# Second self attention: the second part of context, key and value weights filled with zeros to 128 rows

## The reference

```python
HEADS, DIM_HEAD, ATTN_MATRIX_SCALE = 8, 128, 1.5      # context: 2 x 512 rows of 192 features
qh = _split_heads(x @ Wq)                             # Wq 256 x 1024; 8 heads, 2048 x 128 each
kh = _split_heads(context @ Wk)                       # Wk 192 x 1024; 8 heads, 1024 x 128 each
vh = _split_heads(context @ Wv)                       # Wv 192 x 1024
sim = einsum('hid,hjd->hij', qh, kh) * DIM_HEAD ** -0.5
mean = mean(sim, axis=-1)
sim = (sim - mean) * 1.5 + mean
attn = softmax(sim, axis=-1)
out = einsum('hij,hjd->hid', attn, vh)                # heads side by side: 2048 x 1024
x = x + out @ Wout + bout
```

## Time and profile before

| what | value |
|---|---|
| median of three runs | 3127.7 us (3121.81 to 3133.32) |
| profiled execution, its span | 3124.2 us; no time is recorded for it beside the span |
| this part, its own block | from about 1627 us to about 2308 us of the span |
| TensorE busy | 2720.5 us, 87% |
| VectorE busy | 1999.9 us, 64% |
| ScalarE busy | 1747.3 us, 56% |
| GpSimd busy | 792.9 us, 25% |

### The profile page before, as it was taken

One profiled execution on the slowest core, in us unless ns is written; L12 is line 12 of the kernel. 1 busy time (PEld: TensorE's weight loads), 2 busy tenths in 40 slices (PEclk: granted clock), 3 DMA queues, 4 the chain that ended last, 5 costly groups with the idle time before them and its releaser, 6 DMA issues. The chain is left out here.

```text
span 3124.2 us, 50399 instructions
## 1 busy us (share of the span) xinstructions
PE 2720.5 (87%) x17384; PEld 2036.1 (65%) x17384; DVE 1999.9 (64%) x4360; ACT 1747.3 (56%) x3237; POOL 792.9 (25%) x887
## 2 busy tenths in 40 slices
PE   6778888888876689999979999999979999949998
PEld 3344444444435556777658888888867777748887
DVE  4788778778865756655646666666666556545444
ACT  3888887878874444444435555555555555542221
POOL 1122212222210134444432111111005566610000
PEclk8789889988878899999999999999989999969999
DMA  3000000000001111111010000000010000020000
GB/s 102 4 4 4 0 3 3 0 3 3 1 1 52 68 46 24 24 29 42 21 34 13 6 6 3 6 1 1 1 66 8 8 5 5 2 95 7 3 7 30
DMA packets 88677, 57.76 MB, mean 18 GB/s; under 512 B 55120, under 2 KB 78544, under 8 KB 88016
## 3 DMA queue, kind: packets, MB, share of 16 engines
q1 hardware_dynamic: 88528, 55.80, 6.0%
HBM read 39.00 MB, written 8.39 MB: 15 GB/s over the span
## 5 line engine op out<-in xcount | busy, mean ns | idle before, releaser
L672 DVE SCALAR_TENSOR_TENSOR a_w<-a_w,a_sinks 128x384 f32<-128x384 f32 x512 | 332.8, 715 | 32.0 <-ACT a_w L507 32.0
L2033 POOL TENSOR_SCALAR x_weights<-x_weights,x_sums 128x256 f32<-128x256 f32 x256 | 231.8, 924 | 275.0 <-DVE x_sums L2092 275.0
L1125 POOL TENSOR_SCALAR f_weights<-f_weights,f_sums 128x256 f32<-128x256 f32 x256 | 232.0, 924 | 272.9 <-DVE f_sums L1355 272.9
L486 ACT ACTIVATE a_e<-psum 128x1024 f32<-128x1024 f32 x192 | 195.4, 1018 | 155.7 <-PE psum L345 114.7
L1283 ACT ACTIVATE f_weights<-psum,f_negmax 128x256 f32<-128x256 f32 x256 | 117.7, 472 | 215.2 <-DVE f_negmax L1349 215.2
L1619 ACT ACTIVATE a_turned_w_hi<-psum 128x512 fp32r<-128x512 f32 x256 | 139.1, 596 | 152.0 <-PE psum L1529 151.9
L687 DVE SCALAR_TENSOR_TENSOR a_w<-a_e,psum 128x512 f32<-128x512 f32 x256 | 162.8, 677 | 92.8 <-ACT a_e L488 88.0
L342 PE MATMUL psum<-a_qT,a_kT_half 32*128 32x512 f32 x512 | 165.8, 727 | 60.4 <-DVE a_w L687 49.3
L488 ACT ACTIVATE a_e<-a_e 128x1024 f32<-128x1024 f32 x192 | 202.9, 1057 | 6.1
L2003 ACT ACTIVATE x_weights<-x_masked_s,x_negmax 128x256 f32<-128x256 f32 x256 | 127.0, 497 | 138.6 <-DVE x_negmax L2084 138.6
L1735 DVE TENSOR_REDUCE a_negmax<-psum 128x1 f32<-128x1024 f32 x128 | 156.7, 1224 | 65.7 <-PE psum L123 61.5
(11 more groups left out here) (361 smaller groups left out, 7725.5 us busy)
## 6 DMA issues: line engine op xcount, KB each, us to landing
f_xnT<-all_xnT_all SPq DMA_DIRECT2D x16, 256.0 KB, 2.3
f_pv_rows<-f_pv SPq DMA_DIRECT2D x8, 512.0 KB, 3.1
f_pv_groups<-f_pv_rows SPq DMA_DIRECT2D x8, 512.0 KB
f_w<-in_f_w SPq DMA_DIRECT2D x2, 2048.0 KB, 10.0
all_x_all<-in_x SPq DMA_DIRECT2D x1, 2048.0 KB, 8.4
a_xnT<-all_xnT_all SPq DMA_DIRECT2D x8, 256.0 KB, 2.3
x_xnT<-all_xnT_all SPq DMA_DIRECT2D x8, 256.0 KB, 2.3
x_ctxT<-in_x_ctxT SPq DMA_DIRECT2D x8, 256.0 KB, 2.7
```

What stands on the lines that cost most here:

```text
L486: act.activation(e[:, x, :], psS[x], ACT.Exp).then_inc(exp_done, 1)
L672: ins = dve.scalar_tensor_tensor(part, part, sinks[:, col:col + 1], part, ALU.is_ge, ALU.mult)
L1125: ins = pool.tensor_scalar(w, w, sums[:, k, h, t:t + 1], None, ALU.mult)
L2033: ins = pool.tensor_scalar(w, w, sums[:, k, h, t:t + 1], None, ALU.mult)
```

## The change

The second chunk of the context, of the key weights and of the value weights is filled up with zeros to 128 partitions. Every product of `project_kv` then takes all 128 rows for both chunks. Sizes in the other direction, the number of instructions on TensorE and their order stay as they are. The zeros of `ctxT` and `wv` are written by GpSimd, behind those of `wraw`. The four writes now stand before GpSimd's wait for the loads, and TensorE waits for them (`blank`) before its first product. The split of the context's second chunk takes 128 rows too.

```diff
@@ block.tensor
             pe.wait_ge(loaded, 16 * len(loads))
+            pe.wait_ge(blank, 1)
...
-                    for c, rows in enumerate((P, CTX - P)):
+                    for c in range(2):
                         if i < 4 and h == 0:
-                            ins = pe.matmul(kv_bank(n), wraw[0:rows, 0, 1, c * AD:(c + 1) * AD],
-                                            ctxT[0:rows, c, i * QUARTER:(i + 1) * QUARTER], start=(c == 0), stop=(c == 1))
+                            ins = pe.matmul(kv_bank(n), wraw[:, 0, 1, c * AD:(c + 1) * AD],
+                                            ctxT[:, c, i * QUARTER:(i + 1) * QUARTER], start=(c == 0), stop=(c == 1))
                         elif i < 4:
-                            ins = split_product(pe, kv_bank(n), [z[0:rows, h % 2, 1, c * AD:(c + 1) * AD] for z in wparts],
-                                                [z[0:rows, c, i * QUARTER:(i + 1) * QUARTER] for z in ctx_parts], c == 0, c == 1)
+                            ins = split_product(pe, kv_bank(n), [z[:, h % 2, 1, c * AD:(c + 1) * AD] for z in wparts],
+                                                [z[:, c, i * QUARTER:(i + 1) * QUARTER] for z in ctx_parts], c == 0, c == 1)
                         else:
                             lo = (2 * (i - 4) + j) * P
-                            ins = pe.matmul(kv_bank(n)[:, j * AD:(j + 1) * AD], ctxT[0:rows, c, lo:lo + P],
-                                            wv[0:rows, c, h * AD:(h + 1) * AD], start=(c == 0), stop=(c == 1))
+                            ins = pe.matmul(kv_bank(n)[:, j * AD:(j + 1) * AD], ctxT[:, c, lo:lo + P],
+                                            wv[:, c, h * AD:(h + 1) * AD], start=(c == 0), stop=(c == 1))
@@ block.scalar
-                    c, rows = n - 4, (P, CTX - P)[n - 4]
-                    act.activation(ctx_parts[0][0:rows, c, :], ctxT[0:rows, c, :], ACT.Copy).then_inc(ctx_high, 1)
+                    c = n - 4
+                    act.activation(ctx_parts[0][:, c, :], ctxT[:, c, :], ACT.Copy).then_inc(ctx_high, 1)
@@ block.gpsimd
+            for par in range(2):
+                pool.memset(wraw[CTX - P:P, par, 1, AD:2 * AD], 0.0)
+            pool.memset(ctxT[CTX - P:P, 1, :], 0.0)
+            pool.memset(wv[CTX - P:P, 1, :], 0.0).then_inc(blank, 1)
             alone(pool, loaded, 16 * len(loads), passed)
-            for par in range(2):
-                ins = pool.memset(wraw[CTX - P:P, par, 1, AD:2 * AD], 0.0)
-            ins.then_inc(blank, 1)
             alone(pool, blank, 1, passed)
@@ block.vector
-                    c, rows = n - 5, (P, CTX - P)[n - 5]
+                    c = n - 5
                     dve.wait_ge(ctx_high, c + 1)
-                    dve.tensor_tensor(ctx_parts[1][0:rows, c, :], ctxT[0:rows, c, :], ctx_parts[0][0:rows, c, :].bitcast(F32),
+                    dve.tensor_tensor(ctx_parts[1][:, c, :], ctxT[:, c, :], ctx_parts[0][:, c, :].bitcast(F32),
                                       ALU.subtract).then_inc(ctx_low, 1)
```

## The result

The changed kernel takes 3097.24 us (median of 4 runs, 3095.03 to 3102.12), the kernel before 3128.21 us (4 runs, 3121.81 to 3133.32). The ratio is 0.9911, with a 95% interval of 0.9888 to 0.9934: 0.9% faster. The prediction said 3099 us, and 28.8 us of gain; the medians lie 31.0 us apart. The profiled span fell from 3124.2 to 3093.4 us.

The account below looks back on a forecast made before the run. The prediction took TensorE to set the loop's pace, busy 525.24 of 540 us. Loop 28.9 and preamble 4.0 - 2.35 - 1.7 = -0.1 sum to 28.8 us gained, so 3127.7 becomes 3099, range 3089 to 3110.

Parts of the forecast that it names:

- Values: Values projections in the loop: 0.69 us too much each for row-count changes, 28 x 0.69 = 19.3 us gained.
- The steps around a change of the row count: Keys projections in the loop: steps around two changes are 0.38 us too long, 28 x 0.38 = 10.6 us gained.
- The second half of the last change: First scores step behind values, 21 places: 0.08 us may stay for fp32 meeting fp32r, 0.02 gained each, 0.4 us.
- Waits for GpSimd: In 13 loop steps TensorE waits; 0.10 us gained in about 7 with keys is waited away, minus 0.7 us.
- The margin of 0.6 us: Elsewhere in the loop GpSimd ends 0.6 us before its reader; shrinks by 0.1 to 0.2 and holds.
- Loop: All terms of the main loop together: 28.9 us gained.
- Preamble: Projections ahead of queries 6, before the first scores: 4 x 0.40 + 3 x 0.79 = 4.0 us gained.
- Fills: GpSimd's zeros ahead of TensorE's first product: 0.92 us for 1024 columns, TensorE starts 2.35 us late.
- The clock: Longer idle before TensorE's first product lowers the granted clock for one stretch: minus 1.7 us, bounds 0 and 3.4.
- The signs: Trace after: no 64-row records in `project_kv`, eight value records 0.88 us, 13 waits each 0.1 longer, low clock at start.
- Absorption: Rival, chance 0.09: ScalarE and VectorE partly set the loop's pace, half its gain, 14.5 us, is left: 3113.
- No gain: Rival, chance 0.07: long steps belong to something that stays, only the late start is paid, 2.35 + 1.7 us: 3131.8.

Follow-up runs that it names:

- fills alone: Changed kernel with all products back on 64 rows in the second chunk, zeros still written and waited for; 3131.05 us, ratio 1.0015 to the kernel before.
- the other order of chunks: Kernel before, without zeros, second block of values taking its chunks in reverse so two 64-row chunks stand together; 3118.12 us, ratio 0.9965.
- 96 rows: Changed kernel with 96 partitions instead of 128 in the second chunk of every product; 3098.43 us, ratio 0.9903 to the kernel before.

## Why the prediction was right

The mechanism was right. The total, 28.8 us where the spans of the two profiles differ by 30.8, came out as close as it did in part by luck, since the terms missed in both directions. Values gave 1.3 us more than predicted, the waits for GpSimd took 1.9 more, and 0.5 of the loop is missing besides. The preamble gave 0.4 more, the start cost 0.1 less, and 1.7 us for the clock weren't paid in this profile. The profile before had a low clock behind the first scores, which the changed one had not, another 0.9.

**The steps around a change of the row count.** Right, and now shown by three kernels: 0.38 us for a projection of keys (1.000 + 0.335 us before, 0.723 + 0.233 after, means over 28). The term of 10.6 us stands, though one of the 28, in the loop's first step, was lost to waits.

**Values.** Mis-sized by little: 0.69 predicted, 0.753 measured (1.566 to 0.813, mean of 21). I took all eight steps at 0.11; seven are, and the eighth, ahead of the scores, is 0.03. At the 7 starts of a head, 2.613 to 2.034, 0.58 instead of 0.59. Together 19.9 us where the sum had 18.6.

**The second half of the last change.** The number was right, its reading wrong. Gained were 0.021 in each of 21 places (0.335 to 0.314), 0.4 us, and 0.08 of the step's length stayed, as behind the transposes. But it is no cost of meeting fp32r products: the step ahead is 0.08 shorter. The transposes of the earlier trace rows show the same, which the prediction read from the step behind alone:

```profile
1793.91 0.27 PE L1529 MATMUL psum<-all_ident,a_weights 128*128 128x128 f32 x1
1793.94 0.36 PE L121 MATMUL psum<-a_wparts_hi,a_oT_hi 128*128 128x256 f32 x1
```

That is 0.03 ahead and 0.20 behind, together the plain 0.11 + 0.12. With both steps counted, the four changes of a values projection gave 0.753 + 0.021 = 0.774 us, 0.19 each, as for keys (0.378 for two). So the 0.08 that I left standing was gained too; my two terms, 0.69 and 0.02, are short by 0.06 together for that reason.

**Waits for GpSimd.** Mis-sized: 0.7 us predicted, 2.6 measured. I had charged 0.10 us in 7 steps behind keys. Both halves of the last change lie behind the projection's last product, for keys 0.09 in front of the scores and 0.10 behind, and the chain of `kv_hi`, `x_hi` and GpSimd starts from that product. So 0.19 us are waited away, behind keys (0.38 to 0.57 us) and behind values too (1.13 to 1.32), and 0.26 in the first of the 13. The margin of 0.6 us held everywhere else.

**Loop.** 10.6 + 19.9 + 0.4 - 2.6 = 28.3 us, and the trace gives 27.8 at equal clock; 28.9 was predicted. Of the 0.5 us between, 0.3 lie in the scores behind keys: from one step's first scores product to the next, a step with keys that has no wait got 0.367 us shorter, and not 0.378, since the steps among those scores are 0.01 longer in all. The rest, 0.2 us, I can't assign.

**Preamble.** 4.4 us, 4.0 predicted. VectorE's split of the context's second chunk took 1.63 us instead of 2.33, with GpSimd's bias additions beside it in both. The number of partitions isn't the reason: it took 2.33 with 128 of them (fills alone) and 1.62 with 64 (the other order of chunks). What is the reason wasn't tested.

**Fills.** 2.33 us late, 2.35 predicted; 1024 columns took 0.95 us, 0.92 predicted.

**The clock.** The term of 1.7 us was right as the price of one stretch, and its bounds of 0 and 3.4 hold all eight profiles. The profile on which the result was read was one without a fall. Taken as certain it was wrong; it is a matter of six in eight.

**The signs.** Long steps in the second chunk are gone, and no new wait stands before `project_q`. TensorE waits 0.4 us before one `turn`, which the first profile of the kernel before doesn't show, but its second does (0.5 us), so it isn't new. Three signs came otherwise than forecast: eight records of values take 0.81 us and not 0.88, the waits grew by 0.19 and not 0.1, and the clock stayed at 1.00.

**Rivals.** Absorption: only the 13 places that waited already, 2.6 us; out. No gain: out, by the order of chunks and by 96 rows. The Trainium skill (TensorE: Matmul & The Clock Gate, LDWEIGHTS), which gives a weight load the time of its columns whatever the contraction, agrees with the equal steps of 64-row, 96-row and 128-row products away from the changes (0.12 us for 256 columns) and with the weight loads of 0.18 to 0.19 us in the lines above, for 64 rows as for 128; it says nothing against a cost between them. Row tiling, which the Trainium skill (TensorEngine Tiling (Array Packing), Performance Considerations) wants for small contractions, wasn't tried.

## What to carry to other kernels

Read TensorE by distances from start to start. Where products of 128 and 64 rows alternate, each change shows as a pair of long steps, 0.2 us in excess together. Where TensorE sets the pace most of this comes back once the small chunk is filled with zeros, here 27.8 of some 32 us in the loop. For values, half of it came back with the order of the chunks alone. Judge an excess by both steps around a place, since one of them can be short by as much as the other is long. Put what the fill costs where its engine is idle and nobody waits. Then look again at the waits that have grown: here they pointed to one call that had to go first on GpSimd, worth 14 us of the loop where the change itself had brought 28.

## What the runs showed of the hardware

- 96 rows behave as 128: no step is longer around them. 64 rows cost about 0.19 us at each change, and the weight load there starts 0.20 us behind the product ahead instead of with it.
- Behind plain fp32 products and transposes the step to the first fp32r product is 0.08 us shorter (0.03 for 0.11) and the step behind that product 0.08 us longer (0.31 for 0.23, 0.20 for 0.12). Together this costs nothing.
- A late start with 3.0 us of idle lowered the granted clock, from 1.00 to means of 0.50 to 0.68 over the next 4 us, in six profiles of eight, for 1.65 to 3.0 us of work. An idle of 0.73 to 0.88 us did so in none of five. But 1.41 us before the first scores did in two of three (before, and fills alone), and 1.6 to 2.1 us in the same place in none of the nine profiles that had it. What decides there is open.
- Twelve waits with 11.4 us of recorded idle gave back 14.1 us when they went.
